# Routing the last sequence in two halves, with its residuals and normalisation on VectorE and its row copies on ScalarE

## The reference

```
x = x + _layernorm(_L0_attn_ref(_layernorm(x)), ...)   # 16 query heads, 4 key/value heads of 64, decay per key feature
x = x + _layernorm(_L0_ffn_ref(_layernorm(x)), ...)    # 8 experts, 2 for each token, inner size 512

logits = einsum('bth,eh->bte', x, router_w) + router_b
topv, topi = top_k(logits, 2);  gates = softmax(topv)
# for each expert e: acc += down(silu(gate(x)) * up(x)) * sum(gates * (topi == e))
```

## Time and profile before

| | |
|---|---|
| median of 3 runs | 1352.33 us (1351.22 to 1353.1) |
| profiled execution, its own time | 1352.28 us |
| its span (first to last instruction) | 1350.0 us |
| mean granted TensorE clock | 0.978 |
| busy: PE, DVE, ACT, POOL | 92%, 58%, 50%, 41% of the span |
| first load of expert rows issued | 913.44 us |

### The profile page before, as it was taken

How to read it: one execution, slowest core, us unless ns; L and a number is a source line. 1 busy time by engine, 2 the same in 40 slices (tenths; PEclk the granted TensorE clock), 3 DMA queues, 4 the chain that set the end, 5 groups by cost and what they waited for, 6 DMA issues and landing times.

```text
span 1350.0 us, 27575 instructions
## 1 busy us (share of the span) xinstructions
PE 1238.0 (92%) x8012; PEld 1035.7 (77%) x8012; DVE 784.3 (58%) x2349; ACT 672.9 (50%) x1711; POOL 558.1 (41%) x683
## 2 busy tenths in 40 slices
PE   3999999999999999999999999718999999999976
PEld 1778778788787787797787887707899999988952
DVE  2667777767767776777777677512333333333327
ACT  2456565565475475565655654403444444444426
POOL 2223644535535436436445354152333333333326
PEclk9999999999999999999999999958999999999998
DMA  7000100100101101101001001213311111111164
GB/s 271 8 17 9 40 16 23 39 12 27 31 14 33 31 8 39 31 8 39 16 23 39 10 21 36 83 51 92 113 49 49 49 49 47 47 47 47 47 217 184
DMA packets 60280, 67.97 MB, mean 50 GB/s; under 512 B 7488, under 2 KB 50144, under 8 KB 59872
## 3 DMA queue, kind: packets, MB, share of 16 engines
q1 hardware_dynamic: 50656, 46.03, 10.6%
q0 software_dynamic: 8448, 17.45, 3.8%
q10 hardware_dynamic: 1152, 4.19, 1.0%
HBM read 38.50 MB, written 29.15 MB: 50 GB/s over the span
## 4 chain that ended last, share of the span: by engine, by line
PE 63%; DVE 13%; issue 9%; DMA 5%; POOL 4%; ACT 4%; DVEq 1%; SPq 0%; POOLq 0%; ACTq 0%
PE pA L555 8%; PE pO L571 8%; PE pO L712 8%; PE pO L573 6%; PE pW L600 4%; PE pA L703 3%; PE pA L704 3%; PE pJ L703 3%; PE pJ L704 3%; PE pT L583 3%; DMA expert_out<-y,tail 2%; POOL expert_rows L1390 2%; PE pJ L489 2%; DVE S_raw L1049 2%; PE pJ L600 2%
## 5 line engine op out<-in xcount | busy, mean ns | idle before, releaser
L1446 POOL DMA_INDIRECT expert_out<-y,tail x136 | 130.2, 958 | 263.4 <-ACT y L958 236.2
L571 PE MATMUL pO<-vJ,aT 128*128 128x128 f32 x1024 | 194.0, 279 | 0.0
L573 PE MATMUL pO<-S_mid,qT 128*128 128x128 f32 x896 | 173.2, 275 | 0.0
L829 ACT ACTIVATE sq<-pO 128x512 f32<-128x512 f32 x128 | 75.8, 592 | 184.7 <-PE pO L571 142.1
L571 PEld LDWEIGHTS pO<-vJ,aT 128*128 128x128 f32 x1024 | 153.8, 192 | 14.6 <-issue 13.2
L1390 POOL DMA_INDIRECT expert_rows<-x1n,rowi x128 | 124.9, 976 | 53.9 <-issue 41.8
L1072 DVE TENSOR_REDUCE ss<-sq 128x8 f32<-128x512 f32 x128 | 86.5, 676 | 101.2 <-ACT sq L829 101.1
L573 PEld LDWEIGHTS pO<-S_mid,qT 128*128 128x128 f32 x896 | 136.0, 192 | 0.0
L555 PE MATMUL pA<-qT,kT 128*128 128x256 f32 x512 | 133.3, 383 | 2.5 <-DVE qT L1033 2.5
L712 PE MATMUL pO<-wdown_sb,vJ 128*128 128x128 f32 x1088 | 132.7, 275 | 0.0
L712 PEld LDWEIGHTS pO<-wdown_sb,vJ 128*128 128x128 f32 x1088 | 126.8, 192 | 0.0
(11 more groups left out here) (215 smaller groups left out, 2628.6 us busy)
## 6 DMA issues: line engine op xcount, KB each, us to landing
xt<-expert_rows SPq DMA_DIRECT2D x69, 130.0 KB, 2.2
xa<-x SPq DMA_DIRECT2D x16, 256.0 KB, 2.8
xr<-x SPq DMA_DIRECT2D x16, 256.0 KB, 2.8
after_attention<-x SPq DMA_DIRECT2D x16, 256.0 KB, 2.4
arena<-after_attention ACTq DMA_DIRECT2D x8, 512.0 KB, 3.6
expert_rows<-zeros SPq DMA_DIRECT2D x8, 390.0 KB, 2.9
expert_out<-y,tail POOLq DMA_INDIRECT x136, 2.2
wgate_sb<-wgate SPq DMA_DIRECT2D x1, 2048.0 KB, 9.1
```

Of the source, the lines that this page charges most:

```text
L571: last = mm(o, aT[:, c % 2, p, h * P:(h + 1) * P], vJ[:, c, p, :], start=True, stop=(c == 0))
L573: last = mm(o, qT[:, p, c, 2 * h:2 * h + 2, :].rearrange("p r c -> p (r c)"), S_mid[:, c, p, :], start=False, stop=True)
L1446: g.indirect_dma_start(out=ys_dram, in_=y[:, k, :], in_offset=None, out_offset=bass.IndirectOffsetOnAxis(ap=tail[:, k, 1:2].bitcast(U32), ...
```

## The change

For the last sequence alone (S - 1 = 15) the routing is cut into `HALVES`, tiles 0 and 1, and tiles 2 and 3. It has rows of its own (`last_rows`, laid over tiles that this turn doesn't use) and row numbers of its own (`last_rowi`), so that its scatters need not wait for those of sequence 14. POOL keeps only the indirect DMAs: the residuals (`last_residual`) and the normalisation (`last_norm`) go to DVE, the second copy (`copy_last_rows`) to ACT. The first half's steps stand inside or right behind chunk 7. `weigh` and `next_goals` of sequence 14 come on DVE after chunk 6 instead of chunk 7. In all sequences `both` is computed before `later`, the rows of numbers before the gates in `weigh`, and the total in `ranks` in a loop of its own; counts of instructions stay the same there.

```diff
@@ PE
             chunks(S - 1, False, True)
+            pe.wait_ge(base_ready, FIRST + S - 1)
+            router_transposes(S - 1, S - 1, last_rows, HALVES[0])
             out_transposes(S - 1, NC - 1)
+            logits(S - 1, HALVES[0])
             merge_heads(S - 1, NT - 1, False)
-            pe.wait_ge(base_ready, FIRST + S - 1)
-            router_transposes(S - 1)
-            logits(S - 1)
-            ranks(S - 1)
+            ranks(S - 1, HALVES[0])
+            pe.wait_ge(base_ready, FIRST + S)
+            router_transposes(S - 1, S, last_rows, HALVES[1])
+            logits(S, HALVES[1])
+            ranks(S, HALVES[1])
@@ ACT, in the chunks
+                    if not more and c == 7:
+                        router_rstd(i, i, HALVES[0])
                     head_scale(i, c)
@@ ACT, behind them
             chunks(S - 1, False, True)
+            router_T(S - 1, HALVES[0])
             out_T(S - 1, NC - 1)
+            copy_last_rows(HALVES[0])
+            router_exp(S - 1, HALVES[0])
             merged_rstd(S - 1, NT - 1)
-            router_rstd(S - 1)
-            router_T(S - 1)
-            act.wait_ge(diff_ready, S)
-            a(ediff[:], diff[:], ACT.Exp).then_inc(ediff_ready, 1)
+            router_rstd(S - 1, S, HALVES[1])
+            router_T(S, HALVES[1])
+            copy_last_rows(HALVES[1])
+            router_exp(S, HALVES[1])
@@ DVE, in the chunks
                     if routed and c == 6:
-                        places(i - 1)
+                        places(i - 1, rowi)
                         if not more:
                             dve.wait_ge(base_ready, FIRST + i)
                             v.tensor_copy(end_i[:], base[:]).then_inc(ends_ready, 1)
+                            weigh(i - 1, x1n[:])
+                            next_goals(i - 1)
                     if c in (4, 6, 7):
                         merged_apply(i, (4, 6, 7).index(c))
+                        if not more:
+                            last_residual((4, 6, 7).index(c))
+                    if not more and c == 6:
+                        router_stats(i, HALVES[0])
...
+            def last_residual(t):
+                dve.wait_ge(an_ready, (S - 1) * NT + t + 1)
+                dve.wait_ge(xr_in, (S - 1) * 16 + 16)
...
+                v.tensor_tensor(x1[:, t, :], an[:, t, :], xr[:, t, :], ALU.add).then_inc(x1_ready, 1)
+
+            def last_norm(n, tiles):
+                dve.wait_ge(r_rstd, n + 1)
+                for t in tiles:
+                    v.tensor_scalar(last_rows[:, 0, t, 0:HID], x1[:, t, :], mv[:, 2, t, 0:1], rstd[:, 2, t:t + 1],
+                                    ALU.subtract, ALU.mult).then_inc(x1n_ready, 1)
@@ DVE, behind them
-            merged(S - 1, NT - 1)
-            router_stats(S - 1)
-            choose(S - 1)
-            weigh(S - 1)
-            places(S - 1)
+            choose(S - 1, S - 1, HALVES[0])
+            merged_stats(S - 1, NT - 1)
+            places(S - 1, last_rowi, HALVES[0])
+            merged_apply(S - 1, NT - 1)
+            last_residual(NT - 1)
+            router_stats(S - 1, HALVES[1])
+            weigh(S - 1, last_rows, HALVES[0])
+            last_norm(S, HALVES[1])
+            choose(S - 1, S, HALVES[1])
+            weigh(S, last_rows, HALVES[1])
+            places(S, last_rowi, HALVES[1])
@@ POOL
-                residual(i, 0)
                 if more:
+                    residual(i, 0)
                     gate_relative(i + 1, 1)
-                residual(i, 1)
-                residual(i, 2)
+                    residual(i, 1)
+                    residual(i, 2)
...
-            residual(S - 1, NT - 1)
-            scattered_all(S - 2)
-            router_norm(S - 1)
-            copy_rows(S - 1)
             pool.wait_ge(pad_out, 16 * (E + 1))
-            scatter(S - 1)
+            for n, tiles in enumerate(HALVES):
+                scatter_last(n, tiles)
```

207 lines of the change are left out of this document (126 added, 81 removed).

## The result

| | before | after |
|---|---|---|
| median of 4 runs | 1352.71 us (1351.22 to 1354.57) | 1334.03 us (1333.46 to 1335.41) |
| ratio | | 0.9864, 95% interval 0.9853 to 0.9876 |
| profiled execution, its span | 1352.28, 1350.0 us | 1333.82, 1332.0 us |
| granted clock, mean | 0.978 | 0.983 |
| last scatter (number 128) starts | 910.66 us | 891.97 us |

The change makes the kernel 1.36% faster, 18.7 us. The forecast was 1333.9. The whole gain lies ahead of number 128: it starts 18.69 us earlier, the load of the first rows stands 2.78 us behind it in both kernels, and from TensorE's first tile of the expert stage to the end it is 434.3 us before and 435.0 after.

The account below looks back on a forecast made before the run. The expert stage's start was taken to wait for POOL's last scatter. Bringing it 17.9 us earlier, plus 0.5 from the loop, gave 18.4 us off 1352.28: 1333.9 us, range 1331.5 to 1339.

Parts of the forecast that it names:

- The sum: From attention to expert stage the last scatter starts 17.9 us earlier; the loop gives 0.5: 18.4 us.
- The step from 113 to 114: POOL, first to second scatter of sequence 14: 5.65 us start to start, kept as before the change.
- The gaps of a group's first DMA: POOL, start of each half of sequence 15's scatters: a gap of 0.45 us, at numbers 121 and 125.
- The wait's explanation: POOL's 4.56 us idle behind sequence 14's first scatter comes after each 113 indirect DMAs, so it stays there.
- The pads: Last pad lands at 880, costing nothing before 883.45; rival: the 4.56 us belong to pads, 1337.8, chance 0.08.
- The wait is gone: Rival: POOL's idle time behind sequence 14's first scatter vanishes; last scatter at 890.8, time 1331.9; chance 0.07.
- The second half's slack: Sequence 15: DVE's row numbers end at 886.1, POOL reaches number 125 at 888.8; 1.9 us of delay are free.
- The chain from the last residual to the second half's row numbers: Sequence 15's second-half routing across engines: 8.2 us from 877.9, row numbers at 886.1.
- DVE's new work: Sequence 15's residual and normalisation on DVE: 0.36 us a residual, 0.4 us a tile's normalisation.
- The counts: SP's eight loads of tile counts end at 892.1, hidden 2.9 us before the last scatter lands at 895.0.
- DVE against POOL: Rival: DVE's new SBUF work holds POOL's scatters, costing 0.36 + 0.8 us: 1335.1; chance 0.08.
- The clock in the expert stage: TensorE starts the expert stage at the low clock level as before: nothing gained or lost.

Follow-up runs that it names:

- the run without the wait: Changed kernel plus two awaited spare indirect writes on POOL right ahead of sequence 14's scatters: 1333.85 us, ratio 0.9865.
- All three aids: Changed kernel plus two spare writes before sequence 14's scatters, two matmuls behind the last chunk, seven matmuls ahead of the expert stage: 1334.7 us, ratio 0.9872.

## Why the prediction was right, and where it wasn't

- **The sum.** 17.9 us in the joint and 0.5 in the loop were forecast. The last chunks of sequence 15 run 0.79 us earlier (the last head norm's `sq` at 865.25, 866.04 before), and number 128 a further 17.9 us. Number 113 at 868.07 (868.8 forecast; all but 0.06 of the difference is the loop), 120 at 881.9 (882.05), 121 at 883.14 (883.45), 128 at 891.97 (892.7). The chain and its terms were right. That the time hit the forecast to 0.1 us is luck: the 0.3 us more from the loop, the two terms below and the part behind the first load are each larger than that.
- **Two terms were off and cancelled.** The step from 113 to 114 took 6.21 us, 0.56 more than the 5.65 that I kept, since number 113 took 0.6 us longer to land. The gaps of a group's first DMA, put at 0.45 us with a longer first instruction, didn't come: both halves run on at 0.30. That is 0.6 us less.
- **The wait's explanation fell.** This is the part of the mechanism that was wrong. "I therefore take it for something that comes after each 113 indirect DMAs, whatever else happens" is the step that failed. Its practical part held, since the change leaves the DMAs and their numbers alone. The last words did not: spare writes ahead of the loop leave the waits at the same scatters, and with spare writes in the loop the first one isn't seen and the second isn't 113 behind any visible one. The distances of 113 are real in the kernels without spare writes in the loop: from the loop's first scatter to the wait, from there to the next (in the runs with two spare writes it would fall where POOL waits 3.2 us for `y` anyway, and can't be seen), and from the expert stage's first write to the third, which I had called unexplained and which is 129 + 113 = 242. In all six kernels with spare writes that third one is 113 behind the first write of the expert stage (243 twice, 258, 244 twice, 256).
- **The pads.** They belonged to a rival, and that rival's own form is refuted: without a single pad less, the wait is gone from the scatters when two spare writes stand ahead of them. But pads do hold number 121 once the wait is gone, until 882.4 and not 880 as I wrote. With scatters beside them the last is issued at 877.3 instead of 876.0 and lands later.
- **"The wait is gone".** I priced it at 1331.9. The run in which it is gone gave 1333.85. That price took the pads for landed at 880, where POOL waited until 882.4, and number 125 at 886.9, where it started at 888.09.
- **The second half's slack.** 1.9 us were forecast between DVE's row numbers and POOL's need. The rows show 0.5, and in the run without the wait POOL stands still for DVE 0.6 us longer than usual. The cause is the clock, which I had looked at for the expert stage only: the transposes of the first half stand ahead of chunk 7's on TensorE, the engine idles 2.38 us, the clock falls, the merge takes 1.74 us more. The run with two extra matmuls makes the row numbers 2.0 us earlier. The chain from the last residual to the second half's row numbers was sized right, 7.9 us against 8.2; it is its start that was late, 879.0 and not 877.9.
- **DVE's new work** was priced a little high: a residual 0.29 us (0.36), a normalisation 0.30 (0.4). The head norm started 2.1 us later than before, counted from the loop's end, as forecast (2.1).
- **The counts** are hidden by 1.1 us and not by 2.9: SP's loads took until the last scatter had nearly landed. In one run on the slower chip they were the bound.
- **DVE against POOL.** I gave 0.08 to a disturbance. Eleven operations of 128x512 beside three scatters cost these 0.08 us, and the copies 0.35. The page that speaks for it, "SBUF — State Buffer", section "SBUF: two separate sides", of the Trainium skill, ties it to a copy in the two-port mode. The copies here took 0.43 us each and the additions of the same size 0.69, which fits a faster mode for the copies, but no row names it. If it is that mode, the trace doesn't agree with the page: no scatter waits for a copy to end. If it isn't, the page is neither borne out nor refuted.
- **The clock in the expert stage** is back 7.3 us after the first tile's start in the profile of the changed kernel (pairs of matmuls take 0.60 us from 904.29 on), 6.4 us in the kernel before and 5.4 in the second profile of the changed one. "Nothing gained or lost" was right within what two profiles of one kernel differ by.

So it was right with the chain that it named, but with less room than it thought. The scatters' wait, the row numbers and the pads all allow the last scatter at nearly the same time, and SP's loads of the counts would hold the expert stage once 1.1 us more were gained. That is why the two spare writes and the two matmuls, each alone, gave nothing. All three aids together shortened the joint by some 0.8 us up to the first load of expert rows (47.6 us from POOL's copy of the rows, against 48.4), less than what lies behind it varies.

## What to carry to other kernels

When a stall on the path is removed, look at what ends next before giving it a price: here a wait of 5 us within POOL's row of 16 DMAs was worth next to nothing, since two other chains ended with it. A short piece of work put ahead of TensorE's last busy stretch can cost twice, once as idle time and once as a lower clock in the stretch behind it (here 2.38 us of idle time and a merge 1.74 us longer, both hidden by POOL's row). And a regularity in the numbers of a trace (here 113) may hold for the kernel at hand and still be the wrong rule; adding one event ahead of it, and one in the loop, showed that here. Last, read how much the parts that a change doesn't touch vary between profiles before explaining half a microsecond.

## What the runs showed of the hardware

- POOL's wait of 3 to 5 us between two indirect DMAs is not moved by 1 or 16 indirect DMAs ahead of the loop, is gone from the scatters when two awaited ones stand between loop and scatters, and isn't seen after the loop when each of the loop's turns has one DMA more. What is counted there stays open. Where it is seen, it ends 1.8 to 2.5 us behind the landing of the DMA ahead: start to start 5.65, 6.21, 4.65 and 4.04 us, with landings of 3.8, 4.4, 2.2 and 2.2 us (number 114 before and after, numbers 227 and 242 before).
- With TensorE idle for 2.4 to 2.6 us from about 868 us on, the granted clock fell to 0.50 between 870 and 872 us in each of five profiles, and stayed at 1.00 in the two with 1.9 us of matmuls in that gap. In another run it was 0.93 over 888 to 892, behind a burst of 2.9 us, and at 0.50 again from 892 to 896, where TensorE worked for 2.33 of the 4 us; in a second run the same burst left it at 0.50.
- An indirect DMA more in each turn of the loop made the loop 14.3 us longer in 14 turns, though POOL is busy only 41% of the span in the kernel before.
- One chip of three ran the kernel before 31 us slower at nearly the same granted clock (0.975 to 0.978), with turns of the loop of 54.4 to 56.6 us against 52.6, and in some places with waits of 1 us between dependent small instructions of DVE.
- Beside eight copies (0.43 us each) and three additions (0.69) of 128x512 on DVE, one of POOL's scatters took 1.04 us instead of 0.96, and three of the copies 0.48 to 0.65.
- SP's eight loads of the counts into registers started within 4.0 to 4.6 us of each other in most runs, and within 10.6 us in one on that chip.
